# Softmax sums from a column of ones, a gated output matrix, and two of eight distance copies on ScalarE

## The reference

```python
mod = (silu(c) @ wmod).reshape(16, 6, 1, -1)
sa, ca, ga, sb, cb, gb = (mod[:, k] for k in range(6))     # ga, gb: kept at least 0.25 in size
h = layernorm(x) * (1 + ca) + sa
Q, K, V = (h @ W + b).reshape(b, s, 16, 8).transpose(0, 2, 1, 3)   # for q, k, v
scores = Q @ K.T / sqrt(8) + einsum('bhid,ijd->bhij', Q, rel_table[rel_idx])
ctx = softmax(scores) @ V
x = x + ga * (ctx @ Wo + bo)
h = layernorm(x) * (1 + cb) + sb
x = x + gb * moe(h)            # router: top 2 of 8; each expert silu(h w1 + b1) w2 + b2
```

## Time and profile before

| what | value |
|---|---|
| three runs | 684.81, 684.85, 685.73 us; median 684.85 |
| profiled execution | 685.29 us, span 683.6 us |
| granted TensorE clock, mean of the span | 0.96 |
| busy: PE, DVE, ACT, POOL | 588.5, 507.1, 508.8, 423.3 us |
| ACT: exponentials (x512), their accumulator reads (x512) | 254.2, 100.3 us |
| ACT: copies to PT (x256) | 136.4 us |
| DVE: maxima (x512), copies to stage (x125 and x3) | 185.2, 118.1 and 2.9 us |
| DVE: idle ahead of the copies to stage | 33.9 us |
| attention, first exponential to the last product | 30 to 492 us |

### The profile page before, as it was taken

The page is one execution under the profiler, slowest core; times in us unless marked ns, Lnnn a source line. Parts: engine busy times, 40 slices in busy tenths (PEclk is TensorE's granted clock), DMA queues, the critical chain, the costliest instruction groups (busy, mean ns, idle before and its releaser), DMA issues. The chain is left out here.

```text
span 683.6 us, 17706 instructions
## 1 busy us (share of the span) xinstructions
PE 588.5 (86%) x5108; PEld 439.8 (64%) x5108; DVE 507.1 (74%) x1888; ACT 508.8 (74%) x1578; POOL 423.3 (62%) x543
## 2 busy tenths in 40 slices
PE   5667789999899899899989989978798989999950
PEld 4444556666666566566666656655577979999940
DVE  6788988999999999999999999997565312222127
ACT  4157799999999999999989999998643434444434
POOL 2660655747668687686776966855366765554535
PEclk9777999999999999999999999999999999999975
DMA  5996678778787788778868878874525777565538
GB/s 142 308 230 202 198 235 248 228 235 248 214 245 241 213 252 246 228 219 260 249 208 242 252 213 247 243 236 148 189 82 174 236 234 228 198 217 185 176 97 274
DMA packets 173125, 149.03 MB, mean 218 GB/s; under 512 B 16182, under 2 KB 162642, under 8 KB 173030
## 3 DMA queue, kind: packets, MB, share of 16 engines
q1 hardware_dynamic: 168054, 139.33, 67.9%
q0 software_dynamic: 4544, 8.44, 3.7%
q10 hardware_dynamic: 432, 0.14, 0.1%
HBM read 83.71 MB, written 65.05 MB: 218 GB/s over the span
## 5 line engine op out<-in xcount | busy, mean ns | idle before, releaser
L711 ACT ACTIVATE P<-NS,nmax 128x256 f32<-128x256 f32 x512 | 254.2, 504 | 50.5 <-DVE nmax L1312 49.6
L1312 DVE CUSTOM_DVE_ANT_0 NS<-psS,bias 128x256 f32<-128x256 f32 x512 | 185.2, 417 | 2.3 <-PE psS L950 1.6
L968 PE MATMUL psT<-ident,P 128*128 128x128 f32 x1024 | 140.0, 281 | 8.9 <-ACT PT L722 8.8
L1267 DVE COPY stage<-psDist 128x768 f32<-128x768 f32 x125 | 118.1, 945 | 33.9 <-issue 25.2
L722 ACT ACTIVATE PT<-psT 128x512 f32<-128x512 f32 x256 | 136.4, 586 | 0.0
L968 PEld LDWEIGHTS psT<-ident,P 128*128 128x128 f32 x1024 | 118.2, 145 | 24.0 <-issue 9.8
L778 ACT ACTIVATE F<-psS,b1T 128x256 f32<-128x256 f32 x156 | 65.4, 471 | 86.5 <-PE psS L1061 86.5
L609 POOL DMA_INDIRECT results_d<-y,row_u x78 | 76.0, 974 | 56.7 <-DVE y L1458 40.8
L711 ACT ACTIVATION_READ_ACCUMULATOR P<-NS,nmax 128x1 f32 x512 | 100.3, 196 | 0.0
L950 PE MATMUL psS<-Kst,Qst 32*128 32x256 f32 x512 | 65.9, 336 | 34.7 <-DVE nmax L1312 29.9
L1061 PE MATMUL psS<-xT,w 128*128 128x256 f32 x312 | 80.6, 381 | 0.3 <-DMA w<-in_L_ffn_w_dram 0.3
(11 more groups left out here) (254 smaller groups left out, 1044.2 us busy)
## 6 DMA issues: line engine op xcount, KB each, us to landing
dist_d<-stage SPq DMA_DIRECT2D x128, 384.0 KB, 3.0
bias<-dist_d SPq DMA_DIRECT2D x256, 192.0 KB, 3.3
w<-in_L_ffn_w_dram SPq DMA_DIRECT2D x39, 512.0 KB, 3.7
x<-slots_d SPq DMA_DIRECT2D x39, 129.0 KB, 3.0
y<-results_d SPq DMA_DIRECT2D x16, 256.0 KB, 5.0
dist_d<-zeros SPq DMA_DIRECT2D x1, 2048.0 KB, 14.4
out_dram<-y SPq DMA_DIRECT2D x8, 256.0 KB, 3.2
results_d<-y,row_u POOLq DMA_INDIRECT x78, 3.0
```

The lines of the kernel that those rows point to most:

```text
L711: act.activation(P[:, p % 2, h, q, :], NS[:, p % 2, h, q, :], ACT.Exp, scale=-1.0, bias=nmax[:, p % 2, k:k + 1], accum_out=lsum[:, b % 2, ...
L968: mm = pe.transpose(psT[:, h, S * k + 128 * q:S * k + 128 * q + 128], P[:, p % 2, h, q, 128 * k:128 * k + 128], ident[:])
L1267: dve.tensor_copy(stage[:, p % STAGES, :, :, :], bank[:, :, 0:2 * RW].rearrange("p h (q c) -> p h q c", q=2)).then_inc(dist_out, 1)
L1312: dve.tensor_tensor_reduce(NS[:, p % 2, h, q, :], psS[:, h, S * q:S * q + S], bias[:, p, h, q, :], 1.0, 3e38, ALU.add, ALU.min, nmax[:, p ...
```

## The change

The values' weight tile keeps its 32 columns a head, but the eight zero groups become: eight values, a column of ones, seven zeros. So a `weigh` yields, beside a head's eight unnormalised context rows, the sum of its exponentials. Two groups go to one half of `psO`, the other two to the other half. The exponentials give no accumulator any more.

In step 3 of the next batch ACT copies all 512 columns of `psO` (`copy_values`), PE transposes them in four pieces back into `psO` at that step, ahead of its jobs (`turn_values`; before, the two transposes stood behind step 2's weigh). DVE's `context` moves from behind the jobs of step 3 to directly behind the maxima of step 4: a reciprocal of 32 sums and one product of 256 columns, rows now on the partitions. Job `ct` in step 4 transposes the context back (two transposes), ACT copies it to `ctxT`, and in step 6 the extra job `y` multiplies it by `WoG` in two matmuls, already with rows on the partitions, and DVE adds it to `X`. ACT takes `ct` and `nh` behind the exponentials of step 5.

`WoG` is `Wo` times the batch's gate. A new extra job `gain` in step 7 of the batch itself spreads gate and gated bias over the partitions (two matmuls with a broadcast column of the identity), and DVE takes it with a copy (`boR`) and a product (`WoG`). GpSimd adds `boR` to `X` (`add_bias`) in the next batch behind the third stack; the addition of `y` waits for that. A job `gains`, once, in step 4 of batch 0, transposes the gates and gated biases into `gR`.

In the batches after the first ACT copies the distances in steps 0 and 4, behind `gather`. `Wo` and `bv` are reordered on the host, so that eight small DMAs become two.

```diff
+BY_ACT_OUT = (0, 4)
...
-           (("y", -1), ("nh", 2)), (("u01", -2),), (("u23", -2),), (("q01", 2),))
-X_SLOTS = ((), (("rank", -4),), (("turn", -2),), (("back", -2),), (("tally", 1 - B),), (("rows", -3),), (("t", -1),), ())
+           (("ct", -1), ("nh", 2)), (("u01", -2),), (("u23", -2),), (("q01", 2),))
+X_SLOTS = ((), (("rank", -4),), (("turn", -2),), (("back", -2),), (("gains", 0), ("tally", 1 - B)), (("rows", -3),),
+           (("y", -1),), (("gain", 0),))
...
+def act_puts_out(b, p):
+
+    return b > 0 and p in BY_ACT_OUT and PAIRS * b + p + AHEAD < STEPS
...
-            for a in range(4):
-                at = slice(32 * a, 32 * a + 32)
-                sp.dma_start(WoD[at, :], Wo.rearrange("(g a d) e -> a g d e", a=4, d=D)[a]).then_inc(weights_in, 16)
-                sp.dma_start(bvT[at, :], bv.rearrange("(g a d x) -> a g d x", a=4, d=D, x=1)[a],
-                             allow_slow_non_contiguous=True).then_inc(weights_in, 16)
+            sp.dma_start(WoD[:], Wo).then_inc(weights_in, 16)
+            sp.dma_start(bvT[:], bv.rearrange("(e a) -> e a", a=1)).then_inc(weights_in, 16)
...
+            def add_bias(r):
+                at = slice(2 * r, 2 * r + 2)
+                pool.wait_ge(x_dve, X_TAKEN["gain", r][0])
+                pool.tensor_tensor(X[:, at, :], X[:, at, :], rep(boR[:], 1, 2), ALU.add).then_inc(biased, 1)
...
                     act.activation(P[:, p % 2, h, q, :], NS[:, p % 2, h, q, :], ACT.Exp, scale=-1.0,
-                                   bias=nmax[:, p % 2, k:k + 1],
-                                   accum_out=lsum[:, b % 2, q, a, p // 2:p // 2 + 1]).then_inc(exp_done, 1)
+                                   bias=nmax[:, p % 2, k:k + 1]).then_inc(exp_done, 1)
...
+            def copy_values(b):
+                act.wait_ge(values_done, HG * b + HG)
+                past(act, ctx_full, b)
+                act.activation(C[:], psO[:], ACT.Copy).then_inc(c_copied, 1)
+
+            def put_out(n):
+                act.wait_ge(dist_done, n + 1)
+                act.wait_ge(written[(n - STAGES) % SLOTS], 16 * ((n - STAGES) // SLOTS) + 16)
+                act.activation(stage[:, n % STAGES, :, :, :],
+                               psD[:, :, 0:2 * RW].rearrange("p h (q c) -> p h q c", q=2), ACT.Copy)\
+                    .then_inc(dist_out, 1)
...
                 if p == 3 and b > 0:
-                    sums(b - 1)
+                    copy_values(b - 1)
+                exps(b, p)
                 for name, of in M_OF.get(at, ()):
                     if name in BY_ACT:
                         act.wait_ge(m_full, M_DONE[at][0] + 1)
                         take(name, of, psM)
-                exps(b, p)
                 if (b, p) > (0, 0):
                     gather(*at)
+                if act_puts_out(b, p):
+                    past(act, x_dve, so_far(X_DONE, b, p)[1])
+                    past(act, x_act, so_far(X_DONE, b, p)[2])
+                    put_out(PAIRS * b + p + AHEAD)
...
+                elif name == "ct":
                     pe.wait_ge(ctx_done, b + 1)
-                    mm = pe.matmul(bank[:, 0:S], WoD[:], ctxT[:], start=True, stop=True)
+                    for k in range(2):
+                        mm = pe.transpose(bank[:, 128 * k:128 * k + 128], ctx_r[:, k, :], ident[:])
...
+                elif name == "y":
+                    pe.wait_ge(m_act, M_TAKEN["ct", r][1])
+                    pe.wait_ge(x_dve, X_TAKEN["gain", r][0])
                     for k in range(2):
-                        mm = pe.transpose(spare[:, k, :], yT[:, 128 * k:128 * k + 128], ident[:])
+                        mm = pe.matmul(spare[:, k, :], ctxT[:, 128 * k:128 * k + 128], WoG[:], start=True, stop=True)
...
+                elif name == "gain":
+                    for k in range(2):
+                        mm = pe.matmul(spare[:, k, :], ident[:, r:r + 1].broadcast_to([128, 128]), gR[:, k, :],
+                                       start=True, stop=True)
...
+            def turn_values(b):
+                pe.wait_ge(c_copied, b + 1)
                 for q in range(2):
-                    mm = pe.transpose(psO[:, S + 128 * q:S + 128 * q + 128],
-                                      linvD[:, q, :, :, :].rearrange("p a g d -> p (a g d)"), ident[:])
+                    for r in range(2):
+                        mm = pe.transpose(psO[:, S * q + 128 * r:S * q + 128 * r + 128],
+                                          C[:, S * r + 128 * q:S * r + 128 * q + 128], ident[:])
                 mm.then_inc(ctx_full, 1)
...
+                elif name == "gain":
+                    dve.tensor_copy(boR[:], spare[:, 1, :])
+                    i = dve.tensor_tensor(WoG[:], WoD[:], spare[:, 0, :], ALU.mult)
+                elif name == "y":
+                    dve.wait_ge(biased, r + 1)
                     i = dve.tensor_tensor(X[:, 2 * r:2 * r + 2, :], spare, X[:, 2 * r:2 * r + 2, :], ALU.add)
...
             def context(b):
-                dve.wait_ge(lrow_done, b + 1)
+                values = psO[:].rearrange("p (n m d) -> p n m d", n=4, d=2 * D)
+                dve.wait_ge(ctx_full, b + 1)
+                dve.reciprocal(linv[:], values[:, :, :, D:D + 1].rearrange("p n m d -> p n (m d)")).then_inc(linv_done, 1)
                 if b > 0:
-                    dve.wait_ge(m_full, M_FULL["y", b - 1])
-                dve.tensor_tensor(ctxT[:], psO[:, 0:S], lrow[:], ALU.mult).then_inc(ctx_done, 1)
+                    dve.wait_ge(m_full, M_FULL["ct", b - 1])
+                dve.wait_ge(linv_done, b + 1)
+                dve.tensor_tensor(ctx_r[:].rearrange("p q (r m d) -> p (q r) m d", r=2, d=D), values[:, :, :, 0:D],
+                                  rep(linv[:], 3, D), ALU.mult).then_inc(ctx_done, 1)
...
+                if p == 4 and b > 0:
+                    context(b - 1)
...
-                if p == 0 and b > 0:
-                    inverses(b - 1)
...
-                if n < STEPS:
+                if n < STEPS and not act_puts_out(b, p):
```

More of the change, by code:

```diff
@@ L56 @@
 X_LATE = ()
-BY_ACT = ("y", "nh", "back")
-M_LAST = (("logits", B - 3), ("y", B - 1), ("u01", B - 2), ("u23", B - 2), ("logits", B - 2), ("u01", B - 1),
+BY_ACT = ("ct", "nh", "back")
+M_LAST = (("logits", B - 3), ("ct", B - 1), ("u01", B - 2), ("u23", B - 2), ("logits", B - 2), ("u01", B - 1),
           ("u23", B - 1), ("logits", B - 1))
-X_LAST = (("turn", B - 2), ("rows", B - 3), ("t", B - 1), ("back", B - 2), ("turn", B - 1), ("rank", B - 3),
+X_LAST = (("turn", B - 2), ("rows", B - 3), ("y", B - 1), ("back", B - 2), ("turn", B - 1), ("rank", B - 3),
           ("rows", B - 2), ("back", B - 1), ("rows", B - 1), ("rank", B - 1))
@@ L73, in list_jobs @@
                     if 0 <= b + shift < B and (name != "rank" or (b + shift) % 2)
-                    and (name != "tally" or b == B - 1)]
+                    and (name != "tally" or b == B - 1) and (name != "gains" or b == 0)]
             done[b, p] = full, dve, act
@@ L351, in attention @@
             sm("turned"), sm("pt_done"))
[L352 to L354 removed]
+        values_done, ones_in, biased = sm("values_done"), sm("ones_in"), sm("biased")
+        dist_done, dist_out, linv_done, ctx_full, c_copied, ctx_done = (
+            sm("dist_done"), sm("dist_out"), sm("linv_done"), sm("ctx_full"), sm("c_copied"),
             sm("ctx_done"))
@@ L697, in _ @@
             act.wait_ge(zeros_done, 1)
-            act.activation(V[:].rearrange("p b k g a h d -> p (b k g) (a h d)"), rep(zeros[:], 1, 16), ACT.Copy)\
+            act.activation(V[:].rearrange("p b k g a c d -> p (b k g) (a c d)"), rep(zeros[:], 1, 16), ACT.Copy)\
                 .then_inc(v_zero, 1)
-            act.activation(lrow[:, 0:1], zeros[:, 0:1], ACT.Exp)
+            act.activation(C[:, 0:1], zeros[:, 0:1], ACT.Exp)
             def exps(b, p):
@@ L729, in take @@
                 else:
-                    i = act.activation(yT[:], bank[:, 0:S], ACT.Identity, scale=modT[:, 2, b:b + 1],
-                                       bias=gabo[:, b:b + 1])
+                    i = act.activation(ctxT[:], bank[:, 0:S], ACT.Copy)
                 i.then_inc(m_act, 1)
@@ L737, in squash @@
                 act.activation(th[:, at, :], z[:, at, :], ACT.Tanh, scale=0.5).then_inc(squashed, 1)
-            def sums(b):
-                act.wait_ge(ctx_full, b + 1)
-                past(act, ctx_done, b)
-                act.activation(lrow[:], psO[:, S:2 * S], ACT.Copy).then_inc(lrow_done, 1)
+            def copy_values(b):
[8 more added lines that the diff above has]
+                    .then_inc(dist_out, 1)
             def back(r, src):
@@ L797, in _ @@
             for b in range(B):
-                if b == 1:
-                    act.wait_ge(taken, 3)
                 for p in range(PAIRS):
@@ L803, in _ @@
             act.activation(p1[:, 0:1], ident[:, 0:1], ACT.Silu)
-            sums(B - 1)
-            act.wait_ge(m_full, M_FULL["y", B - 1])
-            take("y", B - 1, banks[1])
```

(16 more changed lines are left out.)

64 lines of the change are left out of this document (25 added, 39 removed).

## The result

The changed kernel takes **701.12 us** (median of four runs, 698.82 to 702.44) where the kernel before takes 685.02: a ratio of **1.0226, 95% interval 1.0199 to 1.0253**. The forecast was 690.2; its sign was right, its size a third of the 16 us measured, and its range (to 696) did not reach. The profiled execution took 702.44 (span 700.7, that is 17.1 over the span of before).

What follows compares the result with a forecast made beforehand. Pace set step by step, by PE's own work and DVE's chain from step 7. Plain intervals +0.23 (eight, 1.8), choosing +0.6 (six, 3.6), start -1.2, batch 0 +0.6, closing +0.6: +5.4 on 684.85, 690.2 us; range 681 to 696.

Steps and rivals of the forecast that it cites:

- The plain interval: One batch's ctxT product to the next, without the top-2 choice on DVE (eight, 26.65 us each): +0.23 us each.
- S1-S2: Start of step 1's score matmuls to step 2's: -0.17 us at most in plain intervals, from relieving DVE in step 0.
- the gain's take: DVE's copy and product between put_out(7) and the maxima of step 0: +0.40 us, bounds 0.25 and 0.65.
- The turned values: Four transposes ahead of the logits, between the score starts of steps 4 and 5: +0.32 us.
- S6-S7: Score start of step 6 to step 7, plain intervals: ACT's relief and the output product cancel, 0; bounds -0.1 and +0.2.
- Rival 1: ACT sets the plain intervals, so relieving it makes the kernel faster: -5 us, about 680; chance 0.20.
- Rival 2: Nothing measurable: the gain's 0.40 is hidden because DVE reaches step 7 sooner, 684.7 us; chance 0.17.
- Rival 3: The exp keeps its 0.49 us (700), or ACT's copy holds PE in steps 1 and 5 of every batch (697); chance 0.13.
- the choosing interval: One batch's ctxT product to the next, holding the top-2 choice on DVE (six, 29.29 us each): +0.6 us each.
- S7-S0: Score start of step 7 to that of step 0: 0 in both kinds of interval.
- The rank product's +0.2: Choosing intervals, step 1: PE's rank job waits for ACT's copy of step 0's distances, +0.2 us, between 0 and 0.4.
- The closing: Kernel's end, bias addition ahead of the last normalisations: +0.6 us, of it +0.3 the addition and 0.33 the matmul pair.

Runs made afterwards that it cites:

- experiment 9: Changed kernel with only the gain job taken off VectorE (ScalarE copies both rows, GpSimd multiplies Wo): 692.31 us, 1.0104 of the kernel before.
- experiment 3: Changed kernel with all copies of distances on VectorE again, none on ScalarE: 699.95 us, 1.0209 of the kernel before.
- the other edits: Changed kernel with chosen behind step 7's maxima, ScalarE's step 0 copy in even batches only, last bias addition late: 691.86 us; with gain off VectorE too, 678.18.
- experiment 4: Changed kernel with the last batch's bias addition on GpSimd put behind batch 14's second normalisation and its multiply: 698.12 us, 1.0176 of the kernel before.
- before again: The kernel before, unchanged, run for a second profile: 685.01 us.
- experiment 6: Changed kernel in which ScalarE copies step 0's distances in even batches only, VectorE in odd ones: 692.34 us, 1.0140 of the kernel before.
- experiment 5: Changed kernel with chosen in its place but written as two comparisons with a constant, one SBUF input each: 694.29 us, 1.0164 of the kernel before.
- experiment 2: Changed kernel with the gain job moved from step 7 to step 0 of the next batch: 697.22 us, 1.0186 of the kernel before.

## Why the prediction was wrong

**Right.** The plain interval: +0.15 against +0.23, with its relief in S1-S2 (-0.17, as forecast) and the gain's take in the chain from step 7 to step 1 (+0.43 in S7-S1, +0.40 forecast; experiment 9 takes 0.40 back out of S0-S1). No accumulator rows are left on ACT, four exps take 1.71, and the first maxima come 1.55 sooner (1.2 forecast). The turned values and the smaller job in their place were put at +0.32 and -0.32 and came to +0.18 and -0.08. S6-S7 was put at 0, as ACT's relief of 0.43 against 0.33 for the output product and a wait of 0.1, and fell by 0.23, beyond its bound of -0.1. That these three misses cancel, and the sum comes within 0.08, is in part luck.

Rival 1, ACT, is out: its busy time fell from 26.12 to 25.14 in a plain interval, S6-S7 gave 0.23, and the interval still grew, by what stands in VectorE's chain. The rule of the Trainium skill that I set beside it (Perfetto Trace Analysis, Identifying the Most-Contended Engine), to optimise the engine of the highest occupancy first, gave the wrong sign here. Rival 2 is out, too: the gain's 0.40 was not hidden. Rival 3 named the time, 700, but by a chance of numbers: its exponentials that keep their 0.49 did not come (0.40 now). Its other half, ACT's copy that holds PE, came only for the rank product in choosing intervals; in plain ones S1-S2 fell.

**The step that failed** is the sum of the choosing interval, "0.32 - 0.32 + 0.40 + 0.2 = +0.6": it was 1.73.
- It has no term for S7-S0. I priced VectorE's instructions by their durations and took those as fixed, and set GpSimd's part at "nothing", as busy 19.81 of 26.65 and waiting for nothing. `chosen` went from 0.21 to 1.09 because ScalarE's relief, which I had counted only for TensorE's waits, brought GpSimd's multiply 0.37 forward: +0.87 in that step, of which 0.64 in each of the first five choosing intervals is shown to come back without it. That GpSimd comes sooner by ScalarE's relief is read from the rows; it comes as soon without ScalarE's copies (experiment 3: 3.78 behind the maximum, `chosen` 1.09), and no run puts the accumulators back.
- The rank product's +0.2 (bounds 0 and 0.4) was +0.59 in its step, +0.57 without the sixth interval. The mechanism was right and the size was off: by my own sum, 2.3 against 1.97, it was 0.33, of which I took 0.2. ScalarE's copy takes 0.80 and not 0.7, and the product comes 2.43 behind S1; that is 0.46 over the 1.97. Its pair lasts 0.41 in place of 0.30, which is the other 0.11.
- The gain's 0.40 was right for its own step, but off VectorE it gives 0.90 alone and 1.03 with the other edits (first five intervals), since GpSimd's phase goes with it.

**Two smaller terms.** The closing, put at +0.6 with "+0.3" of it for the bias addition, was +2.34: I counted the instruction, not its wait of 1.07 for WoG with the normalisation queued behind it, nor the clock drop; experiment 4 shows both. The stretch behind the closing, put at 0, was +3.79.

**What stays open.** That last stretch goes with the granted clock: over the 100 us behind the last context product it is 1.00 in three profiles (before, before again, experiment 6), where the stretch lasts 191.9 to 192.3, 0.98 in seven (193.0 to 194.6) and 0.97 in three (195.2 to 195.7, the changed kernel among them). Why the clock falls is open: the drop at 537 follows TensorE's wait of 2.51 for `earlier` (L1389), but the kernel before has the same wait there (2.53) at clock 1.00, and in experiment 6 it is 2.54 with clock 1.00 and the stretch is 191.93 long. So I cannot say what lets the clock fall in the other runs. The +1.36 of batch 0 lies well within its scatter over variants with the same work there (50.36 in experiment 5, 55.09 in experiment 4), and there, too, the clock differs: up to batch 1's maxima(4) it is 0.89 in the first, 0.86 in the second.

## What to carry to other kernels

The duration of a VectorE instruction between SBUF tensors can hold only for the GpSimd instruction that it met: before a change shifts the two against each other, look up each VectorE row between SBUF tensors that lasts several times its column count's worth, or whose neighbour on GpSimd starts within a microsecond. When a relieved engine gives nothing back in one kind of interval, split the edit by kind: here ScalarE's copies gain 0.65 in one and lose 0.44 in the other. Read the clock of every interval before averaging: one of six, at another clock, moved the mean by up to 0.4. And small takes on the engine whose chain sets the pace are worth moving even to two other engines: 0.56 us of VectorE work moved gave 0.35 in a plain interval and 1.03 in a choosing one, most of the step from a kernel 1.0% slower to one 1.3% faster than before.

## What the runs showed of the hardware

Some VectorE instructions on SBUF tensors that start while GpSimd works on SBUF tensors end just behind GpSimd's: `chosen` (1.09 for 0.21) 0.08 behind it, `ahead_of` (1.06 for 0.42) 0.29. Not all do: `bn_stats`, which reads SBUF, keeps its 0.26 to 0.30. The maxima and the copies to `stage`, which read PSUM, show no such growth beside GpSimd's instructions (0.43 and 0.96 at most). The Trainium skill (SBUF — State Buffer, Who interferes with whom) states it as an exclusive lock on a port pair that these two engines share, held for a whole instruction, for VectorE instructions with two SBUF inputs or in a two-port mode; the rows agree on the block for `chosen` and `ahead_of`, which have two, and on GpSimd's being held in turn (1.35 for 1.27).

TensorE's granted clock fell behind an idle stretch of 2.76 us (0.63 over the next four, so partly at 1.2 GHz) and not behind one of 1.57 in the same place; behind 2.5 us, in another place, it fell in some executions and not in others. In experiment 2 it fell behind idle stretches of 1.66 and 1.67 in the choosing intervals of batches 6, 8 and 12, and not behind the same 1.66 in that of batch 10.
